# A two-layer Perceiver on one core: the second layer's three blocks run tile by tile side by side, and its fp4 weights are prepared during the first layer

## The chip, the cores and the metric

The kernel runs as one program on one core of a Trainium2 chip. Times are device microseconds (us) of that core. The core has TensorE (PE in the profile, with PEld for its weight loads), VectorE (DVE), ScalarE (ACT), GpSimd (POOL) and SyncE (SP), which here only issues transfers. Each engine executes its own instructions in the order in which the program was written; what couples the engines are semaphores. SBUF is the working memory, PSUM (8 banks of 128 partitions by 512 fp32) takes what TensorE computes.

## What is computed

The latents are 16 sequences of 64 rows of 256 numbers; seen as rows they are 1024, held in `lat` as 8 tiles of 128 rows (two sequences each). The context is 16 sequences of 1024 rows of 256. All attentions have 16 heads of depth 16.

```python
x = x + cross0(layernorm(x), ctx, mask)      # keys and values from the 1024 context rows
x = x + linear_attention(layernorm(x))       # prefix sums of feature maps
x = x + int8_ffn(layernorm(x))
x = x + cross1(layernorm(x), ctx)            # the same without a mask
x = x + causal_attention(layernorm(x))       # over the 64 rows of a sequence
x = x + fp4_ffn(layernorm(x))

# causal_attention: per head softmax(QK^T * scale, causal) V; then
scrambled = cat.transpose(0, 2, 1).reshape(b, s, e)     # cat: the heads side by side
return scrambled @ W_O
# fp4_ffn, with fp4_quant_dequant in blocks of 16 along the last dimension of x and w:
h = silu(q(x) @ q(w_gate).T) * (q(x) @ q(w_up).T)       # 704 wide
return q(h) @ q(w_down).T
```

`q(x)`: scale = max|block|/6, the quotient is rounded to one of the 15 fp4 values and multiplied by the scale again. All blocks work within a sequence, so a tile of two sequences can pass through causal attention and feed-forward as soon as its own cross attention is done.

## The kernel before, in words

Six blocks run one after the other: cross attention of layer 0 (0 to 514 us of the trace), linear attention (to 641), int8 feed-forward (to 706), cross attention of layer 1 (to 1217), causal attention (to 1326), fp4 feed-forward (to the end). Each block is written as one loop per engine.

**Cross attention** (`cross_attention`) is 64 steps s, four to a batch (a context sequence). A step covers four heads of the batch: scores of two half steps into PSUM banks 0 to 3 (`scores`, L502), maxima (DVE, L687), exponentials (ACT, L630), reciprocal of the sums (DVE, L707), multiplication by it (POOL `normalise`, L429), and one step later the transposes of the probabilities in two parts (`transposes`, L512), which ACT (`take_t`, L649) and DVE (L596) copy out in halves. Beside it TensorE projects values two steps ahead (`project_v`, L477, taken by DVE at L660) and keys four steps ahead (`project_k`, L465, taken by ACT at L608); every second step multiplies probabilities by values (`times_v`, L529). Every eight steps, at s = 10, 18, ..., a latent tile is complete: output projection (`output`, L539) and addition into `lat` (DVE, L712).

**PSUM banks.** All of that except the scores goes through banks 4 to 7 in rotation: `cross_plan` walks the steps in TensorE's order and gives each result the next bank. TensorE may write into a bank only once the engine that reads the result four places earlier in the rotation has taken it.

**Fp4 weights.** In layer 1's cross attention DVE also quantises the three feed-forward weights, one of 8 instructions at each of the steps 4 to 33 (with gaps, L174 to L182, 0.7 to 2.0 us each).

**Causal attention and fp4 feed-forward.** `causal_attention` normalises all eight tiles, then goes tile by tile; its scores are computed over 128 keys, those of both sequences of the tile (2048 logits per row and, after masking, half of them zero). `fp4_ffn` normalises and quantises all tiles in two halves, multiplies the weights by their scales on POOL, transposes them on TensorE (36 transposes), and then goes tile by tile: gate and up (L1812), silu (ACT, L1736), product (DVE, L1696), quantisation of the hidden 704 numbers (DVE, L174 to L182 and L1674), six transposes (L1792), down (L1802), addition and store.

## Time and profile before

| | us |
|---|---|
| median of 3 runs | 1435.48 |
| the runs | 1435.47 to 1437.66 |
| the profiled execution | 1439.74 |
| its span in the trace | 1437.8 |
| TensorE busy | 1300.0 (90%) |
| VectorE busy | 939.4 (65%) |
| ScalarE busy | 784.8 (55%) |
| GpSimd busy | 656.6 (46%) |
| layer 1's cross attention | 706 to 1217 |
| causal attention | 1217 to 1326 |
| fp4 feed-forward | 1326 to 1437.8 |

How to read it: the span is the time from the first to the last instruction of the profiled execution; that execution was 2 us longer than its span. The shares are averages over all blocks. The time of a step of cross attention is read from the starts of the score matmuls (L502). PEclk is the clock that TensorE was granted, as a share of 2.4 GHz. A matmul of fp32 leaves two records in the trace for each matmul of the program. A record's duration includes overlap with its neighbours, so paces are taken from the starts of groups that follow each other.

### The profile page before, as it was taken

To read this page: it belongs to the slowest core of one execution; us is meant where nothing else is said; L and a number is where in the kernel's file an instruction comes from. 1 tells how busy PE (TensorE), PEld (TensorE's weight loads), DVE (VectorE), ACT (ScalarE), POOL (GpSimd) and SP (SyncE) were. 2 spreads that over 40 slices of the span, in tenths; PEclk is the share of its full clock that TensorE was granted. 3 is DMA by queue.
4 is the path that set the end of the run, shared out by engine and by line. 5 is a ranking of instruction groups with operands and counts; after the bars stand their busy time and mean duration, and the time that the engine had idled before them with its cause. 6 is when DMAs were issued, how large, how long until landed. Compare 5 with 4: busy or idle time off the path is not lost. (4 is left out here: it accounts for less than half of the span.)

```text
span 1437.8 us, 27154 instructions
## 1 busy us (share of the span) xinstructions
PE 1300.0 (90%) x10721; PEld 895.3 (62%) x10722; DVE 939.4 (65%) x1670; ACT 784.8 (55%) x1315; POOL 656.6 (46%) x351
## 2 busy tenths in 40 slices
PE   6999999999999966965599999999999997897697
PEld 3676676666666644642256666766667665696465
DVE  4656655666556755957657768676566566586886
ACT  4675666666666623534366666666666664354311
POOL 2755566656666522400145556565555555440200
PEclk9999999999999988987699999999999998899798
...
GB/s 159 76 58 45 45 45 45 87 47 45 45 45 45 1 102 0 1 1 0 108 37 31 51 30 31 80 31 31 31 59 31 31 1 24 4 1 1 0 11 19
DMA packets 17085, 55.29 MB, mean 38 GB/s; under 512 B 2753, under 2 KB 8897, under 8 KB 12737
## 3 DMA queue, kind: packets, MB, share of 16 engines
...
## 5 line engine op out<-in xcount | busy, mean ns | idle before, releaser
L429 POOL TENSOR_TENSOR ca_prob<-ca_prob,ca_inv_sum 128x1024 f32<-128x1024 f32 x256 | 493.4, 1948 | 378.4 <-DVE ca_inv_sum L707 378.4
L608 ACT ACTIVATE ca_kT<-bank,ca_bk 64x512 f32<-64x512 f32 x256 | 174.6, 682 | 223.4 <-PE bank L465 221.6
L512 PEld LDWEIGHTS bank<-ident,ca_prob 128*128 128x128 f32 x2048 | 238.4, 141 | 89.4 <-issue 65.7
L512 PE MATMUL bank<-ident,ca_prob 128*128 128x128 f32 x2048 | 266.7, 274 | 9.0 <-POOL ca_prob L429 7.0
L465 PE MATMUL bank<-ca_ctxT,ca_wk 128*128 128x512 f32 x512 | 244.4, 602 | 17.4 <-DMA ca_bk<-in_L_xattn_bk 17.4
L477 PE MATMUL bank<-ca_wv,ca_ctxT 128*128 128x256 f32 x1024 | 254.5, 392 | 0.0
L684 DVE CUSTOM_DVE_ANT_0 ca_neg_logit<-bank,ca_mask_add 128x1024 f32<-128x1024 f32 x128 | 151.6, 1222 | 131.6 <-PE bank L502 95.0
L477 PEld LDWEIGHTS bank<-ca_wv,ca_ctxT 128*128 128x128 f32 x1024 | 184.6, 190 | 82.2 <-issue 62.5
L687 DVE TENSOR_REDUCE ca_neg_max<-bank 128x1 f32<-128x1024 f32 x128 | 150.7, 1219 | 103.3 <-PE bank L502 103.3
L630 ACT ACTIVATE ca_prob<-ca_neg_logit,ca_neg_max 128x1024 f32<-128x1024 f32 x128 | 146.9, 1150 | 62.8 <-DVE ca_neg_max L684 62.8
L630 ACT ACTIVATE ca_prob<-bank,ca_neg_max 128x1024 f32<-128x1024 f32 x128 | 142.5, 1114 | 63.8 <-DVE ca_neg_max L687 63.8
L596 DVE COPY ca_probT<-bank 128x512 f32<-128x512 f32 x256 | 163.7, 681 | 0.7 <-PE bank L512 0.6
L502 PE MATMUL bank<-ca_kT,ca_q_blk 32*128 32x512 f32 x1024 | 146.0, 640 | 2.8 <-DVE ca_v L660 2.7
L649 ACT ACTIVATE ca_probT<-bank 128x512 f32<-128x512 f32 x256 | 139.1, 595 | 14.3 <-PE bank L512 11.3
L465 PEld LDWEIGHTS bank<-ca_ctxT,ca_wk 128*128 128x128 f32 x512 | 89.7, 194 | 84.2 <-issue 66.6
L529 PEld LDWEIGHTS bank<-ca_probT,ca_v 128*32 128x32 f32 x4096 | 108.9, 111 | 49.5 <-issue 32.3
L529 PE MATMUL bank<-ca_probT,ca_v 128*32 128x128 f32 x4096 | 126.2, 276 | 2.9 <-ACT ca_probT L649 2.9
L660 DVE TENSOR_TENSOR ca_v<-bank,ca_bv 128x512 f32<-128x512 f32 x128 | 87.8, 687 | 54.3 <-PE bank L477 54.2
L502 PEld LDWEIGHTS bank<-ca_kT,ca_q_blk 32*128 32x128 f32 x1024 | 40.1, 183 | 30.6 <-issue 28.3
L411 POOL TENSOR_TENSOR ca_q_blk<-q,small 128x512 f32<-128x512 f32 x32 | 33.3, 1040 | 52.7 <-DVE q L668 52.7
L1450 POOL TENSOR_TENSOR sa_q8T<-sa_qT,small 128x2048 f32<-128x2048 f32 x8 | 28.8, 3610 | 41.1 <-PE bank L1488 32.4
L421 POOL TENSOR_SCALAR ca_mask_add<-ca_mask_i 128x1024 f32<-128x1024 int32 x16 | 44.3, 2770 | 0.0
...
## 6 DMA issues: line engine op xcount, KB each, us to landing
...
```

What stands on the lines that cost most here:

```text
L429: pool.tensor_tensor(prob[:, x, :], prob[:, x, :], inv_sum[:, x:x + 1].broadcast_to([P, CTX]), ALU.mult).then_inc(norm_ready, 1)
L465: mm = pe.matmul(bank[:, x, :], wk[:, k, m * P:(m + 1) * P], ctxT[:, b % 2, k, half * HALF_CTX:(half + 1) * HALF_CTX], start=(k == 0), sto ...
L477: mm = pe.matmul(bank[:, x, r * D:(r + 1) * D], ctxT[:, b % 2, k, ch * P:(ch + 1) * P], wv[:, k, :], start=(k == 0), stop=(k == KD - 1))
L502: mm = pe.matmul(bank[:, 2 * j + half, :], q_blk[rows, b % 2, u, :, :], kT[rows, b % 2, u, :], start=True, stop=True, tile_position=(S * h ...
L512: tr = pe.transpose(bank[:, x, n * P:(n + 1) * P], prob[:, 2 * (s % 2) + p, (4 * h + n) * P:(4 * h + n + 1) * P], core.ident[:, :])
L529: mm = pe.matmul(bank[32 * j:32 * j + 32, x, 0:P], v[:, b % 2, ch, m * P + 32 * j:m * P + 32 * j + 32], probT[:, n % 2, ch, j, :], start=( ...
L596: copy(probT[:, n % 2, 4 * h:4 * h + 4, j, :], bank[:, x, :].rearrange("p (n q) -> p n q", q=P)).then_inc(taken[x], 1)
L608: op = act.activation(kT[half * S:(half + 1) * S, b % 2, 2 * m + r, :], bank[r * S:(r + 1) * S, x, :], ACT.Identity, bias=bk[r * S:(r + 1) ...
L630: act.activation(prob[:, y, :], source, ACT.Exp, bias=neg_max[:, y:y + 1], scale=-1.0 if masked else 1.0, accum_out=row_sum[:, y:y + 1]).t ...
L649: take_t(act, lambda out, x: act.activation(out, x, ACT.Copy), s - 1, 1)
L684: dve.tensor_tensor_reduce(neg_logit[:, p, :], scores, mask_add[:, b % 2, :], -1.0, BIG, ALU.add, ALU.min, neg_max[:, y:y + 1]).then_inc(m ...
L687: dve.tensor_reduce(neg_max[:, y:y + 1], scores, AX.X, ALU.max, negate=True).then_inc(max_ready, 1)
```

## The change

The program has three parts now. `first_layer` is cross attention 0 together with everything that the fp4 weights need: DVE quantises the weights at steps 4, 20 and 36 and the seven following, POOL multiplies by the scales eight steps after that start, and TensorE transposes at the steps 10 to 12 after it, three groups of four for each weight. Linear attention and int8 feed-forward stay as they are. `second_layer` is one loop of 82 steps on each engine, of which 0 to 63 are those of the cross attention. `tile_at(s, lag)` gives the latent tile that passes through a stage at step s: tile t is at lag n in step 10 + 8t + n. The stages by lag:

- 0: cross output, addition, statistics of the normalisation (`TileNorm`; ACT takes the root, DVE finishes it in the next step, in front of `take_v`); 1: transposes for causal attention
- 2: q, k, v; POOL spreads the queries. 4: scores and logits, distances from the maximum on POOL. 5: exponentials. 6: transposes. 7: times values, back transposes, division. 8: output and addition, statistics for the feed-forward's normalisation (in step s % 8 == 2 of the next tile; the quantisation of x stands at lag 9)
- 10: transposes for the feed-forward. 11: gate, up, silu, product. 12 and 13: quantisation of the hidden numbers in two parts, then scaling on POOL. 14: six transposes. 15: down, addition, store.

So the last tile passes through its stages in steps 66 to 81, when no cross attention is left beside it. All results of these stages share banks 4 to 7 with the cross attention; `Banks.open` hands out the next bank when TensorE comes to it, and the rule is the one of before (the result four places earlier must have been taken). Causal attention computes only the 64 keys of a row's own sequence: 1024 logits per row in place of 2048, scores and output in TensorE tiles of 64 rows. ScalarE now goes from the exponential to the root, back, to silu and back in each tile: the program has 40 table loads where it had 13. Layer 1's query projections are at steps 28 and 29, and the mask has one buffer instead of two.

In the program order of VectorE, where latent tile 0 becomes complete (end of step 10; L707 is the reciprocal of the sums, L712 the addition, L687 the maxima, L660 the values), stood before:

```order
L660 TENSOR_TENSOR ca_v<-bank,ca_bv 128x512
L596 COPY ca_probT<-bank 128x4x128 x2
L707 RECIPROCAL ca_inv_sum<-ca_row_sum 128x2
L712 TENSOR_TENSOR lat<-bank,lat 128x256
L687 TENSOR_REDUCE ca_neg_max<-bank 128x1 x2
L660 TENSOR_TENSOR ca_v<-bank,ca_bv 128x512
```

and for a later tile stands now, from the same reciprocal on (L663 the addition, L625 the maxima, L607 the values; `tn` is the tile normalisation, `sa` causal attention, `ff` feed-forward):

```order
L663 TENSOR_TENSOR lat<-bank,lat 128x256
L1482 BN_STATS ca_tn_stats<-lat 128x6 x2
L1486 BN_AGGR ca_tn_mv<-ca_tn_stats 128x2 x2
L1488 TENSOR_SCALAR ca_tn_var<-ca_tn_mv 128x2
L625 TENSOR_REDUCE ca_neg_max<-bank 128x1 x2
L1498 RECIPROCAL ca_tn_rstd<-ca_tn_std 128x2
L1501 TENSOR_TENSOR ca_tn_fix<-ca_tn_rstd 128x2
L1503 TENSOR_TENSOR ca_tn_fix<-ca_tn_fix,ca_tn_var 128x2
L1505 TENSOR_SCALAR ca_tn_fix<-ca_tn_fix 128x2
L1507 TENSOR_TENSOR ca_tn_rstd<-ca_tn_rstd,ca_tn_fix 128x2
L1511 TENSOR_SCALAR ca_sa_xn<-lat,ca_tn_mv,ca_tn_rstd 128x256
L1511 TENSOR_SCALAR ca_ff_x<-lat,ca_tn_mv,ca_tn_rstd 128x256
```

The maxima of the next step stand behind five statistics instructions, and seven more stand between them and the values L607, which are the next row.

On TensorE an even step of layer 1's cross attention was, from its scores to the next ones:

```order
L502 MATMUL bank<-ca_kT,ca_q_blk 128x512 x4
L529 MATMUL bank<-ca_probT,ca_v 32x128 x32
L477 MATMUL bank<-ca_wv,ca_ctxT 128x256 x4
L512 MATMUL bank<-ident,ca_prob 128x128 x8
L465 MATMUL bank<-ca_ctxT,ca_wk 128x512 x2
L512 MATMUL bank<-ident,ca_prob 128x128 x8
```

and a step with s % 8 == 0 is now, with the first rows of the step after it (L498 transposes the probabilities of the cross attention, L1595 those of causal attention, L1795 the hidden numbers, L1611 multiplies by the causal values):

```order
L488 MATMUL bank<-ca_kT,ca_q_blk 128x512 x4
L515 MATMUL bank<-ca_probT,ca_v 32x128 x32
L449 MATMUL bank<-ca_wv,ca_ctxT 128x256 x4
L1595 MATMUL bank<-ident,ca_sa_prob 128x128 x4
L1795 MATMUL bank<-ident,ca_ff_hid 128x128 x5
L1795 MATMUL bank<-ident,ca_ff_hid 64x128
L498 MATMUL bank<-ident,ca_prob 128x128 x8
L1595 MATMUL bank<-ident,ca_sa_prob 128x128 x4
L437 MATMUL bank<-ca_ctxT,ca_wk 128x512 x2
L498 MATMUL bank<-ident,ca_prob 128x128 x8
L488 MATMUL bank<-ca_kT,ca_q_blk 128x512 x4
L1611 MATMUL bank<-ca_sa_probT,ca_sa_value 32x64 x32
```

The hidden transposes stand in front of the cross attention's own, and four more results go through the rotation of banks in this step.

GpSimd had the multiplication by the inverse sums and, every fourth step, the queries of the next batch:

```order
L429 TENSOR_TENSOR ca_prob<-ca_prob,ca_inv_sum 128x1024 x2
L411 TENSOR_TENSOR ca_q_blk<-q_1,small 128x512
L429 TENSOR_TENSOR ca_prob<-ca_prob,ca_inv_sum 128x1024 x8
L411 TENSOR_TENSOR ca_q_blk<-q_1,small 128x512
L429 TENSOR_TENSOR ca_prob<-ca_prob,ca_inv_sum 128x1024 x8
```

and has now (L425 the multiplication, L408 the queries, L1688 the spread queries, L1695 the distances, L1876 the scaling of the hidden numbers):

```order
L1688 TENSOR_TENSOR ca_sa_q<-ca_sa_qk,small 128x1024
L425 TENSOR_TENSOR ca_prob<-ca_prob,ca_inv_sum 128x1024 x6
L408 TENSOR_TENSOR ca_q_blk<-ca_q,small 128x512
L1695 TENSOR_TENSOR ca_sa_prob<-ca_sa_prob,ca_sa_top 128x1024
L425 TENSOR_TENSOR ca_prob<-ca_prob,ca_inv_sum 128x1024 x2
L1876 TENSOR_TENSOR ca_ff_hid<-ca_ff_hid,ca_ff_scale 128x704
L425 TENSOR_TENSOR ca_prob<-ca_prob,ca_inv_sum 128x1024 x6
```

The core of the diff:

```diff
+    def open(self, pe, key, bank=None):
+        if bank is None:
+            bank = 4 + self.turn % 4
+            self.turn += 1
+        wait(pe, self.taken[bank], self.count[bank])
+        self.count[bank] += 1
+        self.at[key] = (bank, self.count[bank])
+        return bank
...
+FW_STEPS = (4, 20, 36)
...
+                if 1 <= s <= STEPS:
+                    ca.transposes(pe, s - 1, 0)
+                if s + 4 < STEPS:
+                    ca.project_k(pe, s + 4)
+                if 1 <= s <= STEPS:
+                    ca.transposes(pe, s - 1, 1)
+                for x in range(3):
+                    if 10 <= s - FW_STEPS[x] < 13:
+                        ffn_weights.transposes_on_tensor(pe, x, s - FW_STEPS[x] - 10)
...
+                    ca.queries(pool, s // GROUPS + 1)
+                for x in range(3):
+                    if s == FW_STEPS[x] + 8:
+                        ffn_weights.scale_on_pool(pool, x)
...
+                for x in range(3):
+                    if 0 <= s - FW_STEPS[x] < 8:
+                        ffn_weights.step_on_vector(dve, x, s - FW_STEPS[x])
...
+    def finish_on_vector(self, dve, j, free):
+        c = self.slots(j)
+        dve.wait_ge(self.std_ready, j + 1)
+        dve.reciprocal(self.rstd[:, c], self.std[:, c]).then_inc(self.fix_step, 1)
+        dve.wait_ge(self.fix_step, 5 * j + 1)
+        dve.tensor_tensor(self.fix[:, c], self.rstd[:, c], self.rstd[:, c], ALU.mult).then_inc(self.fix_step, 1)
+        dve.wait_ge(self.fix_step, 5 * j + 2)
+        dve.tensor_tensor(self.fix[:, c], self.fix[:, c], self.var[:, c], ALU.mult).then_inc(self.fix_step, 1)
+        dve.wait_ge(self.fix_step, 5 * j + 3)
+        dve.tensor_scalar(self.fix[:, c], self.fix[:, c], -0.5, 1.5, ALU.mult, ALU.add).then_inc(self.fix_step, 1)
+        dve.wait_ge(self.fix_step, 5 * j + 4)
+        dve.tensor_tensor(self.rstd[:, c], self.rstd[:, c], self.fix[:, c], ALU.mult).then_inc(self.fix_step, 1)
+        dve.wait_ge(self.fix_step, 5 * j + 5)
+        for y in range(c.start, c.stop):
+            free[y](j - y)
+            dve.tensor_scalar(self.outs[y][:, :], self.core.lat[:, j - y, :], self.mv[:, y, 0:1], self.rstd[:, y:y + 1],
+                              ALU.subtract, ALU.mult).then_inc(self.xn_ready[y], 1)
...
+    def output(self, pe, t):
+        self.banks.wait_taken(pe, ("sb", t))
+        x = self.banks.open(pe, ("sy", t))
+        scrambled = self.cat[:, :].rearrange("p (r u) -> p u r", u=4)
+        for u in range(4):
+            for c in range(2):
+                rows = slice(S * c, S * (c + 1))
+                mm = pe.matmul(self.core.bank[rows, x, 0:D], scrambled[rows, u, :], self.w_o[rows, u, :],
+                               start=(u == 0), stop=(u == 3), tile_position=(S * c, S * c))
...
+    def quantise_hidden(self, dve, t, part):
+        if part == 0:
+            for a in range(2):
+                self.banks.wait_taken(dve, ("fu", t, a))
+            dve.wait_ge(self.x_ready, t + 1)
+        steps = fp4_steps(self.hid[:, :], FB, self.mag[:, :], self.scale[:, :], self.inv[:, :], self.hid[:, :],
+                          self.e[:, :])
+        for n in range(4 * part, 4 * part + 4):
+            steps[n](dve).then_inc(self.h_step, 1)
+            dve.wait_ge(self.h_step, 8 * t + n + 1)
+    def scale_hidden(self, pool, t):
+        pool.wait_ge(self.h_step, 8 * (t + 1))
+        grid, scale = fp4_scaled(self.hid[:, :], self.scale[:, :], FB)
+        pool.tensor_tensor(grid, grid, scale, ALU.mult).then_inc(self.h_ready, 1)
...
+def tile_at(s, lag):
+    n = s - 10 - lag
+    return n // 8 if n >= 0 and n % 8 == 0 and n // 8 < TILES else None
...
+            for s in range(END):
+                if s < STEPS:
+                    ca.scores(pe, s)
+                if (t := tile_at(s, 4)) is not None:
+                    sa.scores(pe, t)
+                if s % 2 == 0 and 4 <= s < STEPS + 3:
+                    ca.times_v(pe, s // 2 - 2)
+                if (t := tile_at(s, 7)) is not None:
+                    sa.heads(pe, t)
+                if (t := tile_at(s, 8)) is not None:
+                    sa.output(pe, t)
+                if s + 2 < STEPS:
+                    ca.project_v(pe, s + 2)
+                if (t := tile_at(s, 2)) is not None:
+                    sa.project(pe, t)
+                if (t := tile_at(s, 6)) is not None:
+                    sa.transposes(pe, t, 0)
+                if (t := tile_at(s, 10)) is not None:
+                    ff.latent_transposes(pe, t)
+                if (t := tile_at(s, 11)) is not None:
+                    ff.project(pe, t, 0)
+                if (t := tile_at(s, 14)) is not None:
+                    ff.hidden_transposes(pe, t)
+                if 1 <= s <= STEPS:
+                    ca.transposes(pe, s - 1, 0)
+                if (t := tile_at(s, 6)) is not None:
+                    sa.transposes(pe, t, 1)
+                if s + 4 < STEPS:
+                    ca.project_k(pe, s + 4)
+                if (t := tile_at(s, 7)) is not None:
+                    sa.back(pe, t)
+                if (t := tile_at(s, 11)) is not None:
+                    ff.project(pe, t, 1)
+                if (t := tile_at(s, 15)) is not None:
+                    ff.down(pe, t)
+                if 1 <= s <= STEPS:
+                    ca.transposes(pe, s - 1, 1)
+                if s in Q_STEPS:
+                    ca.project_q(pe, 1, Q_STEPS.index(s))
+                if (t := tile_at(s, 1)) is not None:
+                    sa.latent_transposes(pe, t, attn_xn)
...
+            ca.queries(pool, 0)
+            ca.add_output_bias(pool)
+            for s in range(END):
+                if (t := tile_at(s, 2)) is not None:
+                    sa.spread_queries(pool, t)
+                if s < STEPS:
+                    ca.normalise(pool, s)
+                if s % GROUPS == 2 and s // GROUPS + 1 < B:
+                    ca.queries(pool, s // GROUPS + 1)
+                if (t := tile_at(s, 4)) is not None:
+                    sa.distances(pool, t)
+                if (t := tile_at(s, 13)) is not None:
+                    ff.scale_hidden(pool, t)
...
+            for s in range(END):
+                if s < STEPS:
+                    ca.maxima(dve, s)
+                if s >= 11 and s % 8 == 3 and (s - 11) // 8 <= TILES:
+                    norm.finish_on_vector(dve, (s - 11) // 8, (attn_free, ffn_free))
+                if (t := tile_at(s, 4)) is not None:
+                    sa.logits(dve, t)
+                if s % 2 == 0 and 4 <= s < STEPS + 3:
+                    ca.take_pv(dve, s // 2 - 2)
+                if (t := tile_at(s, 8)) is not None:
+                    sa.take_output(dve, t)
+                if s + 2 < STEPS:
+                    ca.take_v(dve, s + 2)
+                if (t := tile_at(s, 2)) is not None:
+                    sa.take_value(dve, t)
+                if 1 <= s <= STEPS:
+                    ca.take_t_on_vector(dve, s - 1, 0)
+                if (t := tile_at(s, 6)) is not None:
+                    sa.take_transposed_on_vector(dve, t)
+                if s < STEPS:
+                    ca.inverses(dve, s)
+                if (t := tile_at(s, 7)) is not None:
+                    sa.divide(dve, t)
+                if (t := tile_at(s, 11)) is not None:
+                    ff.hidden(dve, t)
+                if (t := tile_at(s, 9)) is not None:
+                    ff.quantise_x(dve, t, ffn_xn)
+                for part in range(2):
+                    if (t := tile_at(s, 12 + part)) is not None:
+                        ff.quantise_hidden(dve, t, part)
+                if (t := tile_at(s, 15)) is not None:
+                    ff.take_output(dve, t)
+                if s == Q_STEPS[1]:
+                    ca.take_q_on_vector(dve, 1)
+                if (t := tile_at(s, 0)) is not None:
+                    ca.take_output(dve, t)
+                if s >= 10 and s % 8 == 2 and (s - 10) // 8 <= TILES:
+                    j = (s - 10) // 8
+                    if j < TILES:
+                        banks.wait_taken(dve, ("o", j))
+                    if j >= 1:
+                        banks.wait_taken(dve, ("sy", j - 1))
+                    norm.stats_on_vector(dve, j)
...
-        cross(core, 0)
+        fp4 = Fp4Weights(core, sb_in(ctx))
+        first_layer(core, fp4)
         with ExitStack() as layer0:
-            weights = Int8Weights(core, sb_in(layer0))
-            linear_attention(core, weights)
-            int8_ffn(core, weights)
-        weights = Fp4Weights(core, sb_in(ctx))
-        cross(core, 1, weights)
-        causal_attention(core)
-        fp4_ffn(core, weights, out)
+            int8 = Int8Weights(core, sb_in(layer0))
+            linear_attention(core, int8)
+            int8_ffn(core, int8)
+        second_layer(core, fp4, out)
```

## Rows read from the trace of the kernel before

**Rows 1.** The page: busy us, share of the span and instructions by engine.
```profile
PE 1300.0 (90%) x10721; PEld 895.3 (62%) x10722; DVE 939.4 (65%) x1670; ACT 784.8 (55%) x1315; POOL 656.6 (46%) x351
```
**Rows 2.** Stretches: length, busy us of PE, PEld, DVE, ACT, POOL; PEclk, DMA.
```profile
735.00:1208.00 473.00, 469.32 (x4247) 323.24 (x4248) 318.15 (x475) 302.47 (x506) 269.69 (x144) 1.00 0.10 35
1217.00:1326.00 109.00, 92.05 (x794) 79.96 (x795) 76.81 (x97) 47.94 (x67) 33.52 (x11) 0.92 0.04 10
...
1340.00:1358.00 18.00, 9.24 (x30) 6.12 (x31) 17.00 (x20) 4.90 (x11) 0.00 (x0) 0.63 0.00 0
1358.00:1438.00 80.00, 70.13 (x271) 47.66 (x270) 58.87 (x88) 13.88 (x34) 0.00 (x0) 0.93 0.04 14
```
**Rows 3.** Timeline of PE, steps 10 and 11: start, duration, idle before in brackets.
```profile
803.11 1.14 PE L502 MATMUL bank<-ca_kT,ca_q_blk 32*128 32x512 f32 x8
...
808.77 1.88 PE L465 MATMUL bank<-ca_ctxT,ca_wk 128*128 128x512 f32 x4
810.49 1.04 PE L512 MATMUL bank<-ident,ca_prob 128*128 128x128 f32 x8
...
812.32 1.14 PE L502 MATMUL bank<-ca_kT,ca_q_blk 32*128 32x512 f32 x8
...
818.57 1.16 PE L512 MATMUL bank<-ident,ca_prob 128*128 128x128 f32 x8 [0.59 <-DVE ca_v L660]
819.66 1.14 PE L502 MATMUL bank<-ca_kT,ca_q_blk 32*128 32x512 f32 x8
```
**Rows 4.** Timeline of PE: scores of steps 34, 42 and 63.
```profile
987.09 1.14 PE L502 MATMUL bank<-ca_kT,ca_q_blk 32*128 32x512 f32 x8
...
1047.18 1.14 PE L502 MATMUL bank<-ca_kT,ca_q_blk 32*128 32x512 f32 x8
...
1199.98 1.14 PE L502 MATMUL bank<-ca_kT,ca_q_blk 32*128 32x512 f32 x8
```
**Rows 5.** Groups of instructions, 735 to 1208 us: count, busy us, mean ns, idle before.
```profile
L429 POOL TENSOR_TENSOR ca_prob<-ca_prob,ca_inv_sum 128x1024 f32<-128x1024 f32 x128 | 253.7, 2003 | 203.3 <-DVE ca_inv_sum L707 203.3
L687 DVE TENSOR_REDUCE ca_neg_max<-bank 128x1 f32<-128x1024 f32 x128 | 150.7, 1219 | 103.3 <-PE bank L502 103.3
L660 DVE TENSOR_TENSOR ca_v<-bank,ca_bv 128x512 f32<-128x512 f32 x62 | 42.5, 686 | 28.4 <-PE bank L477 28.4
```
**Rows 6.** Timeline of PE in causal attention, one tile's part.
```profile
1277.46 1.95 PE L1488 MATMUL bank<-sa_kT,sa_q8T 128*128 128x128 f32 x16
1279.25 1.04 PE L1524 MATMUL bank<-ident,sa_prob 128*128 128x128 f32 x8
1280.12 1.20 PE L1499 MATMUL bank<-sa_w_o,sa_cat_pad 128*128 128x256 f32 x4
1281.16 1.04 PE L1524 MATMUL bank<-ident,sa_prob 128*128 128x128 f32 x8
```
**Rows 7.** Timeline of PE in the fp4 feed-forward, from tile to tile.
```profile
1403.03 0.82 PE L1792 MATMUL bank<-ident,ff_hq 128*128 128x128 f32 x6
...
1411.40 0.82 PE L1792 MATMUL bank<-ident,ff_hq 128*128 128x128 f32 x6
```
**Rows 8.** Groups of instructions, 1326 to 1438 us.
```profile
L181 DVE SCALAR_TENSOR_TENSOR ff_hid<-ff_hid,ff_h_e 128x704 f32<-128x704 f32 x8 | 7.1, 893 | 0.3
L179 DVE TENSOR_SCALAR ff_h_e<-ff_hid 128x704 int32<-128x704 int32 x8 | 4.2, 527 | 0.3
```
**Rows 9.** Timeline of DVE and POOL at a weight's quantisation.
```profile
785.47 1.74 DVE L177 TENSOR_TENSOR ca_fw_raw<-ca_fw_raw,ca_fw_inv 128x1536 f32<-128x1536 f32 x1
785.63 5.18 POOL L429 TENSOR_TENSOR ca_prob<-ca_prob,ca_inv_sum 128x1024 f32<-128x1024 f32 x2 [3.02 <-DVE ca_inv_sum L707]
```
**Rows 10.** Timeline of PE in the feed-forward's first transposes.
```profile
1349.20 1.94 PE L1759 MATMUL bank<-ident,ff_xq 128*128 128x128 f32 x8 [7.27 <-DVE ff_xq L1674]
```

**Rows 11.** Timeline of ACT before the feed-forward's first silu.
```profile
1351.18 1.09 ACT L1714 ACTIVATE xnT<-bank 128x512 f32<-128x512 f32 x2 [8.57 <-PE bank L1759]
1352.28 1.28 ACT L1736 ACT_TABLE_LOAD   x1
```

1660 lines of the change are left out of this document (845 added, 815 removed).

## The prediction, made before the run

> **What bounds the kernel now.** I read the page's busy shares first: TensorE is busy 90% of the span and no other engine over 65% [rows 1]. Then the windows by block [rows 2]: through layer 1's cross attention TensorE is busy 469 of 473 us at full clock, while DVE is busy 318, ACT 302 and POOL 270. TensorE alone sets the time there, and its gaps total 4 us. In the blocks behind it TensorE is busy 92 of 109 us, 9 of 18 and 70 of 80, and the granted clock falls to 0.63 of full speed in one stretch. The change moves the work of the blocks with gaps into the one without. So the idle TensorE time of those three stretches (17 + 9 + 10 = 36 us, and some of the 14 us between the first two) is all that can be won by overlap; beside it there is work that falls away, and new waits are what can be lost.
>
> The clock of the cross attention is its steps. Eight steps take 1047.18 - 987.09 = 60.1 us [rows 4]; a step that ends with the output projection takes 9.21, 803.11 to 812.32 [rows 3]. One row shows how the rotation of banks bites: at 818.57 TensorE waited 0.59 us for DVE's value copy, in a step of 7.34 us [rows 3]. The values' bank must be free four results later, and DVE had been held by a weight's quantisation.
>
> **The change, part by part.**
>
> *First layer.* It gains 36 weight transposes of 128 columns. The pace is 16 records in 1279.25 - 1277.46 = 1.79 us, 0.11 each [rows 6], so 3.9 us on a TensorE that is as full as in layer 1. DVE's 24 quantisation instructions are the ones that layer 1 had, three POOL multiplications of 1536 elements are new (3 us each by L429's 2.0 for 1024, [rows 5]), and I add 1.4 us for one bank wait and for switches: +5.3 (3.9 if all is hidden, 9 if each weight costs two waits like the one at 818.57). Layer 1 loses that wait: -1.0. Linear attention and int8 feed-forward: 0.
>
> *TensorE work that moves into steps 10 to 62, causal attention, per tile.* 14 transposes at 0.109 = 1.5; 12 records of projections at 0.112 = 1.3; 32 score records of 64 columns at half of 0.112 = 1.8 (0.9 if the two 64-row tiles run side by side); 64 records times values, 0.6; output, 16 records of 256 columns, 1.04 for four [rows 6], in two 64-row tiles side by side, 1.9 (4.2 one after the other). Sum 7.2, and 0.6 for switches between tile shapes: 7.8. *Feed-forward, per tile:* 1411.40 - 1403.03 = 8.37 from tile to tile with TensorE full [rows 7], plus two transposes: 8.6. In steps 10 to 62 fall six causal tiles and the first part (3.4) of a seventh, 50.2, and five feed-forward tiles with gate and up of a sixth (5.1), 48.1. Together 98.3 us, all of it on the path, since TensorE has no gap to take it.
>
> *Waits in those steps.* In the eight-step pattern I followed DVE, ACT and POOL in program order against TensorE's bank requests. DVE waits 103.3 us for score matmuls over 64 steps [rows 5], so it has 1.6 us to spare before the maxima of an average step, and the added groups are longer than that:
> - Step 3 of 8: five statistics instructions and the addition stand before the maxima, about 1 us late; then the finish, five small operations and two of 256 elements, 1.95 us, stands before the values copy (0.69, [rows 5]), whose bank is wanted by the probabilities' transposes: 1.9 us lost.
> - Step 4: quantising x, 3.4 us at the end of step 3, delays the maxima: 0.7.
> - Step 5: the silu needs a table load, 1.28 [rows 11], while it holds the gate's two banks: 0.4.
> - Step 0: the hidden quantisation is five operations like L181's 0.893, two like L179's 0.527 and small ones, 5.5 us in two parts [rows 8]. When DVE works on SBUF operands POOL's multiplication slows: two that normally take 2.0 each [rows 5] took 5.18 together beside a DVE multiplication [rows 9]. POOL has distances (1.9), two multiplications stretched by 0.6 each and then the scaling (1.3) in its queue, and the hidden transposes stand before the cross attention's on TensorE: 1.75.
> - Step 1: the bank of the causal heads waits for ACT, behind the exponentials: 1.2.
>
> Sum 5.95 per eight steps, over six patterns: 35.6 us. Below, it is nothing (every late copy has a bank to spare); above, twice this, 71, if each late operation also delays the next step. I take the walk, since 818.57 shows that a bank wait really falls on TensorE whole. So eight steps become 60.1 + 7.8 + 8.6 + 5.95, about 82.4.
>
> A row on ACT: the load at 1352.28 starts 0.01 us after the copy before it ends and takes 1.28 [rows 11]; no row shows an activation right behind a load. I count 1.28 for each of the four loads per tile.
> By the Trainium skill (ScalarE: Activation LUTs, What ACT_TABLE_LOAD costs), a switch to another set takes about 1.38 us of drain beside the 1.28. By that rule ACT would be 5.5 us busier per tile, and two of these drains would stand before exponentials or the silu that TensorE waits for; the sum would be some 13 us higher. The trace agrees on 1.28 and can't show the rest.
>
> *The tail.* Step 63 starts at 1199.98 [rows 4], and 237.8 us follow before. Now what follows is the last cross steps (about 17 us, as before: causal attention began at 1217, [rows 2]), and then one tile that passes alone through everything. Its chain, from durations of the same operations: normalisation and transposes 5.4, projections to exponential 11.1, to the second addition 6.7, normalisation and quantisation 7.7, gate to product 5.4, hidden quantisation and scaling 6.5, transposes to store 7, so 50, and some 7 for hand-overs. Tile 6's feed-forward stands in the same queues, 16 more. That is 90 with TensorE warm. Cold, eight transposes took 1.94 us [rows 10] against 0.87 warm (1279.25 to 1280.12, [rows 6]), so the 22 us of matmuls in that stretch could double, 112. In the comparable sparse stretch the clock was 0.63 [rows 2], half way: 102.
>
> *Sum.* 1200.0 + 5.3 - 1.0 + 98.3 + 35.6 + 102 = 1440.2 us of span against 1437.8, +2.4. The profiled execution (1439.74) stands 4.3 above the median; on the median's scale the change gives 1435.5 + 2.4, about 1438.
>
> **The rivals.**
>
> *A. The waits are hidden, TensorE stays full.* For it: DVE would be busy some 57 and POOL some 42 of 82 us in eight steps, so nobody but TensorE is near full, and before the waits totalled 4 us in 473 [rows 2]. Against it: the added DVE groups come in lumps of 2 to 3.4 us, over the 1.6 of slack. Price: -35.6, so 1402 on the median's scale; with half of them, 1420.
>
> *B. Slower: late copies chain.* DVE stands late at the maxima in four successive steps (2 to 5), and every maxima 1 us late puts the exponentials, POOL's multiplication and the next step's transposes late as well; POOL's wait for inverses (203.3 us over 64 steps, 3.2 each, [rows 5]) shows that this chain has only little of its step left over. It decides where the lump exceeds 1.6 us in steps without a gap between. The waits would be doubled (+35.6), 1474 on the median's scale, and with half of the doubling 1456. Against it: the odd steps without added work let the queues recover.
>
> *C. Slower: small TensorE tiles don't run side by side.* The rows show eight 32-row records of 512 columns in about 1.1 us [rows 3], against 1.72 for four full ones (808.77 to 810.49, [rows 3]), so 32-row tiles do overlap; no row has 64-row tiles. If they run one after the other, the output costs 2.3 more per tile and the values 0.6 to 3: about 4, over seven tiles 28, so 1466.
> The Trainium skill (TensorEngine Tiling (Array Packing), Key Properties) says tiles operate independently, and that changing the mode drains TensorE. The first half speaks for my 1.9, the second for a larger term than my 0.6 for switches: there are eight to ten changes per tile, and no row here prices one apart from its neighbours.
>
> **How the numbers follow.** My walk: 0.47, centred on 1438, its own range 1422 to 1454 (tail 90 to 112, first layer 3.9 to 9, scores at 0.9). A: 0.28. B: 0.15. C: 0.10. The range reaches from A's 1402 to B's 1474 with little left outside. A comparison of this kernel can't tell differences under about 0.2% (3 us). Faster by more: all of A, 0.28, and the third of my case that lies below 1432.5, 0.15: 0.43. Within 0.2%: 0.14 from my case. Slower: 0.18 from my case, 0.25 from B and C: 0.43.
>
> **What would show it.** In the trace after: eight steps of layer 1 take 82.4 us (76.5 under A, 88 under B); TensorE's idle time there is put down to DVE's values and normalisation in steps 3 and 4, to POOL's scaling in step 0 and to ACT's heads in step 1; 16 causal output records take 1.9 us (4.2 under C); the first layer is 5 us longer; from step 63 to the end it is 102 us with a clock below 0.9. I am wrong in my main step if TensorE is over 98% busy in steps 20 to 60, and in the tail if that lasts under 90 or over 112 us.

## The result and the profile after

The changed kernel takes 1483.59 us (median of 4 runs, 1481.89 to 1485.6) against 1436.47 before in the same comparison: a ratio of 1.0328, 95% interval 1.031 to 1.0346. It is 3.3% slower, outside the range given (1402 to 1474). The profiled execution has a span of 1483.5 us; the forecast was 1440.2 on that scale.

Below are the busy times from the page, then windows with the columns of [rows 2]. The first window is layer 2's loop up to step 63, the second eight steps, the third the tail, the fourth a part of step 44. Where the text names a step 0 to 7, it is the step's number modulo 8, so that step 44 is a step 4:

```profile
PE 1299.6 (88%) x11025; PEld 880.9 (59%) x11026; DVE 968.6 (65%) x1762; ACT 798.5 (54%) x1345; POOL 674.6 (45%) x366
```
```profile
737.00:1377.00 640.00, 590.83 (x5264) 407.29 (x5264) 435.54 (x690) 361.37 (x603) 288.40 (x158) 0.97 0.08 25
1137.00:1226.00 89.00, 81.59 (x724) 56.32 (x722) 62.31 (x97) 48.21 (x82) 37.97 (x22) 0.96 0.08 26
1377.00:1484.00 107.00, 62.16 (x493) 45.20 (x492) 49.79 (x96) 22.68 (x41) 18.43 (x10) 0.71 0.01 4
1168.70:1173.30 4.60, 4.60 (x73) 2.78 (x72) 4.43 (x6) 0.59 (x2) 3.45 (x2) 0.63 0.00 0
```

TensorE had 4 us idle in 473 before [rows 2] and has 49 in 640 now, at a clock of 0.97 in place of 1.00. TensorE's busy total is as before (1300), though causal attention computes half the scores: part of it ran at half clock.

TensorE's timeline of after in eight steps, from step 41 (1137.09) to step 49 (1226.12); it answers to [rows 3, 4]. Start, duration, waits in brackets:

```profile
1137.09 1.14 PE L488 MATMUL bank<-ca_kT,ca_q_blk 32*128 32x512 f32 x8
...
1151.72 2.00 PE L1634 MATMUL bank<-ca_sa_w_o,ca_sa_cat 64*64 64x256 f32 x16
1153.66 1.99 PE L449 MATMUL bank<-ca_wv,ca_ctxT 128*128 128x256 f32 x8
...
1167.20 1.16 PE L498 MATMUL bank<-ident,ca_prob 128*128 128x128 f32 x8 [1.63 <-DVE ca_v L607]
1168.39 0.41 PE L1552 MATMUL bank<-ident,ca_sa_xn 128*128 128x128 f32 x2
1168.73 2.09 PE L488 MATMUL bank<-ca_kT,ca_q_blk 32*128 32x512 f32 x8
...
1177.38 0.41 PE L1774 MATMUL bank<-ident,ca_ff_x 128*128 128x128 f32 x2 [0.74 <-DVE ca_attnT L649]
...
1194.54 2.00 PE L1583 MATMUL bank<-ca_sa_qk,ca_sa_q 64*128 64x64 f32 x32
1196.47 1.95 PE L515 MATMUL bank<-ca_probT,ca_v 128*32 128x128 f32 x64
...
1218.74 0.66 PE L1795 MATMUL bank<-ident,ca_ff_hid 128*128 128x128 f32 x4 [2.15 <-POOL ca_ff_hid L1876]
1220.18 0.69 PE L1795 MATMUL bank<-ident,ca_ff_hid 128*128 128x128 f32 x2 [0.78 <-DVE ca_attnT L649]
1220.87 1.94 PE L498 MATMUL bank<-ident,ca_prob 128*128 128x128 f32 x8
...
1226.12 1.14 PE L488 MATMUL bank<-ca_kT,ca_q_blk 32*128 32x512 f32 x8
```

Eight steps take 89.0 us. The waits in them add to 7.4 (with four smaller ones that aren't shown: 0.84, 0.72, 0.33 and 0.19). Behind two of the waits TensorE ran at half clock: the scores at 1168.73 took 2.09 where the same group at 1137.09 took 1.14, with a granted clock of 0.63 in that window, and eight transposes took 1.94 at 1220.87 in place of 1.04. The wait alone doesn't decide it: of the five waits of 1.63 for the values between 800 and 1320 us only three were followed by slow scores.

Where the time went, by the starts of the score matmuls, forecast beside it: up to step 10 of layer 2 (805.97 against 803.11) +2.9 for +5.3; steps 10 to 63, 571.0 for 396.9, that is +174.1 for 132.9; from step 63 (1376.96) to the end 106.5 for 102. Nearly the whole miss, 41 of 43 us, lies in the steps 10 to 63. Of the 174.1, 98.3 are the forecast TensorE work, 1.7 is a query projection that the change moves in from step 8 (step 8 was 10.07 long before, 8.35 now), and 74.1 are put down to waits and half clock, where the forecast had 35.6. (Some of it is neither: in e1, below, TensorE is busy 77.4 us in eight steps at full clock, and the forecast was 76.5, so about 0.9 per eight steps, some 6 us in all, are work that the forecast lacked.)

Why DVE is late is read in its own timeline at the start of step 4, with GpSimd's instructions beside it:

```profile
1168.24 0.40 DVE L173 TENSOR_REDUCE ca_ff_mag<-ca_ff_x 128x16 f32<-128x256 f32 x1
1168.40 3.75 POOL L425 TENSOR_TENSOR ca_prob<-ca_prob,ca_inv_sum 128x1024 f32<-128x1024 f32 x2 [5.86 <-DVE ca_inv_sum L658]
1168.67 1.65 DVE L174 TENSOR_SCALAR ca_ff_scale<-ca_ff_mag 128x16 f32<-128x16 f32 x1
1170.36 0.25 DVE L175 RECIPROCAL ca_ff_inv<-ca_ff_scale 128x16 f32<-128x16 f32 x1
1170.64 1.78 DVE L176 TENSOR_TENSOR ca_ff_x<-ca_ff_x,ca_ff_inv 128x256 f32<-128x256 f32 x1
1172.46 0.29 DVE L178 TENSOR_SCALAR ca_ff_e<-ca_ff_x 128x256 int32<-128x256 int32 x1
...
1174.38 1.22 DVE L625 TENSOR_REDUCE ca_neg_max<-bank 128x1 f32<-128x1024 f32 x1
```

An operation on 16 numbers took 1.65 us, and one on 256 took 1.78. Alone they take 0.17 and 0.42 (e3, below, has them so), so their work lay behind 1170.15 and behind 1172.00. These points are 1.85 apart, the length of one of GpSimd's two multiplications, and stand 0.12 and 0.15 before the ends of these by the profile (1168.40 + 1.87 = 1170.27, and 1172.15). The reciprocal between them took 0.25, as in e1, so it was not delayed. The quantisation stands right behind the reciprocal of the sums, which releases GpSimd's multiplications: by the order of the program the two always meet. It also goes the other way. Here GpSimd's queries for the next batch, which take 1.04 us where nothing holds them (at 1161.50), take 1.69 beside the last 0.8 us of a DVE multiplication:

```profile
1204.92 2.06 DVE L176 TENSOR_TENSOR ca_ff_hid<-ca_ff_hid,ca_ff_inv 128x704 f32<-128x704 f32 x1
1206.19 1.69 POOL L408 TENSOR_TENSOR ca_q_blk<-ca_q,small 128x512 f32<-128x512 f32 x1
```

The quantisation's operations by their means over the whole kernel after, and the variance of the tile normalisation (count, busy us, mean ns):

```profile
L180 DVE SCALAR_TENSOR_TENSOR ca_ff_hid<-ca_ff_hid,ca_ff_e 128x704 f32<-128x704 f32 x8 | 16.6, 2072 | 0.3
L176 DVE TENSOR_TENSOR ca_ff_hid<-ca_ff_hid,ca_ff_inv 128x704 f32<-128x704 f32 x8 | 14.1, 1768 | 0.3
L179 DVE TENSOR_SCALAR ca_ff_e<-ca_ff_e 128x704 f32<-128x704 f32 x8 | 13.7, 1706 | 0.3
L176 DVE TENSOR_TENSOR ca_ff_x<-ca_ff_x,ca_ff_inv 128x256 f32<-128x256 f32 x8 | 11.5, 1441 | 0.3
L1859 DVE TENSOR_TENSOR ca_ff_hid<-bank,ca_ff_hid 128x352 f32<-128x352 f32 x16 | 8.4, 524 | 34.3 <-PE bank L1784 34.3
L173 DVE TENSOR_REDUCE ca_ff_mag<-ca_ff_hid 128x44 f32<-128x704 f32 x8 | 6.9, 868 | 0.1
L1488 DVE TENSOR_SCALAR ca_tn_var<-ca_tn_mv 128x2 f32<-128x2 f32 x7 | 6.2, 890 | 0.2
```

L180 took 893 ns before (as L181, [rows 8]) and L179 took 527 (as L180, like its neighbour in [rows 8]); now they take 2072 and 1706. The product L1859, which has one operand in PSUM, took 524 also where nothing else was slow (e1), and the reduction took 869 there: these two are not slower. The variance takes 890 ns, where an operation of its form and size (L1505) takes 169: it stands beside GpSimd's queries.

### The profile page after: what moved, and what is told of

Same layout as the page of the kernel before. It is cut to its first block, busy times and chain, and to the rows that moved or that the text cites. A ratio compares the mean times of both kernels' runs of the same rounds, so it can differ in the third digit from the quotient of the medians.

```text
span 1483.5 us, 27972 instructions
## 1 busy us (share of the span) xinstructions
PE 1299.6 (88%) x11025; PEld 880.9 (59%) x11026; DVE 968.6 (65%) x1762; ACT 798.5 (54%) x1345; POOL 674.6 (45%) x366
## 4 chain that ended last, share of the span: by engine, by line
PE 30%; DVE 14%; issue 6%; ACT 2%; DMA 0%; POOL 0%; POOLq 0%; DVEq 0%; SPq 0%; ACTq 0%
PE bank L437 6%; PE bank L498 6%; PE bank L449 4%; DVE ca_neg_max L625 4%; PE bank L488 3%; PE bank L515 2%; PE bank L1784 2%; PE bank L1806 1%; DVE ca_probT L635 1%; DVE ca_v L607 1%; DVE ca_ff_scale L174 1%; PE bank L1634 1%; PE bank L1583 1%; DVE ca_ff_hid L180 1%; DVE ca_ff_e L179 1%
## 5 line engine op out<-in xcount | busy, mean ns | idle before, releaser
L425 POOL TENSOR_TENSOR ca_prob<-ca_prob,ca_inv_sum 128x1024 f32<-128x1024 f32 x256 | 494.7, 1954 | 459.6 <-DVE ca_inv_sum L658 459.6
L498 PEld LDWEIGHTS bank<-ident,ca_prob 128*128 128x128 f32 x2048 | 240.3, 143 | 115.9 <-issue 83.4
L498 PE MATMUL bank<-ident,ca_prob 128*128 128x128 f32 x2048 | 276.0, 278 | 28.9 <-DVE ca_v L607 17.3
L437 PE MATMUL bank<-ca_ctxT,ca_wk 128*128 128x512 f32 x512 | 250.1, 614 | 23.3 <-DMA ca_bk<-in_L_xattn_bk 19.7
L625 DVE TENSOR_REDUCE ca_neg_max<-bank 128x1 f32<-128x1024 f32 x128 | 150.6, 1218 | 89.5 <-PE bank L488 89.1
L607 DVE TENSOR_TENSOR ca_v<-bank,ca_bv 128x512 f32<-128x512 f32 x128 | 87.7, 686 | 44.4 <-PE bank L449 44.3
L408 POOL TENSOR_TENSOR ca_q_blk<-ca_q,small 128x512 f32<-128x512 f32 x32 | 41.0, 1282 | 55.2 <-DVE ca_q L598 55.2
L1688 POOL TENSOR_TENSOR ca_sa_q<-ca_sa_qk,small 128x1024 f32<-128x1024 f32 x8 | 15.2, 1895 | 64.1 <-ACT ca_sa_qk L1651 64.1
```

Source lines behind the costliest of these rows:

```text
L425: pool.tensor_tensor(self.prob[:, x, :], self.prob[:, x, :], self.inv_sum[:, x:x + 1].broadcast_to([P, CTX]), ALU.mult).then_inc(self.norm ...
L437: mm = pe.matmul(self.core.bank[:, x, :], self.wk[:, k, m * P:(m + 1) * P], self.ctxT[:, b % 2, k, half * HALF_CTX:(half + 1) * HALF_CTX], ...
L498: tr = pe.transpose(self.core.bank[:, x, n * P:(n + 1) * P], self.prob[:, 2 * (s % 2) + p, (4 * h + n) * P:(4 * h + n + 1) * P], self.core ...
L625: dve.tensor_reduce(self.neg_max[:, y:y + 1], scores, AX.X, ALU.max, negate=True).then_inc(self.max_ready, 1)
```

## The experiments

Theory H: DVE instructions with two SBUF inputs, and tensor_scalar ones on SBUF, are held until GpSimd's running instruction ends. (Held means: by the profile the instruction has started, and its work comes only later.) The held time makes the maxima and the hidden numbers late. Rival W: DVE is late from the work alone, which comes in lumps longer than its slack. All times are medians: of eight executions for e1, of four for v2_repeat and v3, of two for the others. The kernel before, measured beside each of them, took 1437 to 1441. A waits figure is steps 10 to 63 less 396.9, 98.3 and 1.7, as above.

### e1_reduce: the same work in forms that are not held

```diff
+def fp4_like(x, blocks, mag, scale, inv, y, e):
+    xb = x.rearrange("p (n k) -> p n k", k=HD)
+    half = x[:, 0:blocks // 2 * HD].rearrange("p (n k) -> p n k", k=HD)
+    full = lambda v: v.tensor_reduce(e[:, 0:blocks], xb, AX.X, ALU.max)
+    part = lambda v: v.tensor_reduce(e[:, 0:blocks // 2], half, AX.X, ALU.max)
+    return [
+        lambda v: v.tensor_reduce(mag, xb, AX.X, ALU.max, apply_absolute_value=True),
+        lambda v: v.reciprocal(scale, mag),
+        lambda v: v.reciprocal(inv, scale),
+        full, part, part, full, full,
+    ]
...
-        steps = fp4_steps(self.hid[:, :], FB, self.mag[:, :], self.scale[:, :], self.inv[:, :], self.hid[:, :],
+        steps = fp4_like(self.hid[:, :], FB, self.mag[:, :], self.scale[:, :], self.inv[:, :], self.hid[:, :],
```

> What is changed: in layer 2's tile-by-tile feed-forward the fp4 quantisation of x and of the hidden numbers is replaced by as many DVE instructions of about the same length that are single-input reductions or reciprocals (the numbers are not quantised). Theory H (DVE's two-input and tensor_scalar operations on SBUF are held until GpSimd's running multiplication ends; held time 8 us per eight steps): these forms are not held, eight steps fall from 89.0 to about 83, the time from 1483.6 to about 1449. Rival W (DVE is late only because of the work itself): the same work stands in the same places, time 1475 to 1484.

The kernel doesn't quantise these numbers, so its result is another one.

Measured: 1427.98 us, ratio to before 0.9943 (0.9918 to 0.9968). Its reductions of 704 and 256 numbers and eight steps of its trace:

```profile
L189 DVE TENSOR_REDUCE ca_ff_e<-ca_ff_hid 128x44 f32<-128x704 f32 x24 | 21.3, 886 | 0.8
L189 DVE TENSOR_REDUCE ca_ff_e<-ca_ff_x 128x16 f32<-128x256 f32 x24 | 10.1, 420 | 0.8
```
```profile
1042.00:1131.00 89.00, 86.18 (x816) 61.17 (x807) 59.06 (x106) 51.69 (x87) 38.51 (x22) 1.00 0.08 26
```

The work is as long as the original's unheld durations (886 for 892, 420 for 425), stands in the same places, and TensorE is busy 86 of 89 us again at full clock. Eight steps fell from 89.0 to 80.2, below the 83 that I expected, since the half clock went with the waits. Step 63 starts at 1326.7 in place of 1377.0, and the waits are 22.8 in place of 74.1. So 51 us of the loss in steps 10 to 63 are holds of the quantisation and what they bring, and W is wrong. 22.8 is what my walk, which had 35.6, should be set against. One hold is left in e1: the variance still takes 889 ns, and TensorE's wait for the values in step 3 is still 1.6 us.

### e2_no_quant: the quantisation left out

```diff
-        for n in range(4 * part, 4 * part + 4):
-            steps[n](dve).then_inc(self.h_step, 1)
-            dve.wait_ge(self.h_step, 8 * t + n + 1)
+        if part == 1:
+            dve.wait_ge(self.h_step, 8 * t)
+            dve.reciprocal(self.scale[:, :], self.mag[:, :]).then_inc(self.h_step, 8)
```

> What is changed: the fp4 quantisation of x and of the hidden numbers on DVE is left out (one reciprocal stands for each). Both theories: the waits of steps 4, 7 and 0 go, those of step 3 (normalisation finish, 2.4 us) and step 1 (heads, 1.1) stay; eight steps about 80, and the tail 12 to 15 us shorter: 1420. If H holds, e1 reaches most of the way inside the cross attention (eight steps within 3 us of this one); if W holds, e1 stays 8 us per eight steps above it.

Measured: 1414.08 us, ratio 0.984 (0.9809 to 0.9871). Step 63 starts at 1327.3, 0.6 us from e1's 1326.7. With about 8 us of DVE work more per tile e1 loses nothing inside the cross attention (steps 10 to 63 take 519.7 in both). The 14 us between the two lie behind step 63 (85.9 against 99.9), where the work is on the last tiles' chain.

### e3_before_inverses: the quantisation ahead of the instruction that releases GpSimd

```diff
+                if (t := tile_at(s, 9)) is not None:
+                    ff.quantise_x(dve, t, ffn_xn)
+                for part in range(2):
+                    if (t := tile_at(s, 12 + part)) is not None:
+                        ff.quantise_hidden(dve, t, part)
                 if s < STEPS:
                     ca.inverses(dve, s)
...
-                if (t := tile_at(s, 9)) is not None:
-                    ff.quantise_x(dve, t, ffn_xn)
-                for part in range(2):
-                    if (t := tile_at(s, 12 + part)) is not None:
-                        ff.quantise_hidden(dve, t, part)
```

> What is changed: the same DVE instructions, but the quantisation stands in front of the reciprocal of the sums that releases GpSimd's multiplication, not behind it. H: GpSimd is idle then, nothing is held; the multiplication starts 2.4 to 3.1 us later, which step 4 hides, step 7 does not (about +2) and step 0 half: eight steps about 85, time 1461. W: moving the same work ahead of the reciprocal only adds lateness to GpSimd's chain: 1483 to 1500.

Measured: 1460.4 us, ratio 1.0162 (1.0121 to 1.0204), as H expected (1461): the same instructions, 23 us less than the changed kernel. In its trace:

```profile
L179 DVE TENSOR_SCALAR ca_ff_e<-ca_ff_e 128x704 f32<-128x704 f32 x8 | 12.1, 1515 | 0.3
L180 DVE SCALAR_TENSOR_TENSOR ca_ff_hid<-ca_ff_hid,ca_ff_e 128x704 f32<-128x704 f32 x8 | 7.1, 892 | 0.3
L176 DVE TENSOR_TENSOR ca_ff_hid<-ca_ff_hid,ca_ff_inv 128x704 f32<-128x704 f32 x8 | 7.1, 892 | 0.3
```

Most forms have their own durations again; L179 of the hidden numbers, and with it L178 (1025 ns, where it took 510 in after), still come out long, and I read that as meeting GpSimd's work of the step before. Step 4 fell from 12.95 to 10.1. Step 0 stayed at 13.7 to 15.3: there the hidden transposes still wait for quantisation and scaling.

### e4_hid_late: the hidden transposes at the end of their step

```diff
-                if (t := tile_at(s, 14)) is not None:
-                    ff.hidden_transposes(pe, t)
                 if 1 <= s <= STEPS:
                     ca.transposes(pe, s - 1, 0)
...
+                if (t := tile_at(s, 14)) is not None:
+                    ff.hidden_transposes(pe, t)
```

> What is changed against the changed kernel: the hidden numbers' transposes stand at the end of step 0 on TensorE, behind the cross attention's own (and their copies on ACT behind the cross attention's), nothing else. H (held DVE instructions make the quantisation late, and the transposes that wait for it hold everything behind them): step 0 falls from 14.9 to about 11, since GpSimd's scaling ends before the step does; 5 patterns, 1463. Rival: the exponentials and their chain are late in step 0 anyway and the wait moves to the cross attention's transposes: 1478 to 1484.

Measured: 1481.25 us, ratio 1.0289 (1.0234 to 1.0344): the rival was right. Step 0 is 15.3 long:

```profile
1218.60 0.65 PE L498 MATMUL bank<-ident,ca_prob 128*128 128x128 f32 x4 [3.15 <-DVE ca_attnT L649]
```

The wait has moved to the cross attention's own transposes, whose bank must be freed by a DVE instruction (L649) that stands behind maxima, which stand behind the held quantisation. GpSimd's scaling, which the trace of after names at 1218.74 and on which my step 0 rested, was only the first of two late things. So the 1463 that I drew from H missed.

### e5_pool_halves: how long a hold lasts

```diff
-            pool.tensor_tensor(self.prob[:, x, :], self.prob[:, x, :], self.inv_sum[:, x:x + 1].broadcast_to([P, CTX]),
-                               ALU.mult).then_inc(self.norm_ready, 1)
+            for h in range(2 if self.layer else 1):
+                w = CTX // (2 if self.layer else 1)
+                c = slice(w * h, w * (h + 1))
+                op = pool.tensor_tensor(self.prob[:, x, c], self.prob[:, x, c],
+                                        self.inv_sum[:, x:x + 1].broadcast_to([P, w]), ALU.mult)
+            op.then_inc(self.norm_ready, 1)
```

> What is changed against the changed kernel: GpSimd's multiplication of layer 2's probabilities is issued as four instructions of 512 columns instead of two of 1024. H: a held DVE instruction waits until GpSimd's running instruction ends, so holds halve (256-element multiplication 1.78 us to about 1.1, 704-element 2.06 to about 1.5); 8 us of held time become 4, time about 1463. Rival R (the two engines share a port's rate and slow each other while both run): no instruction of DVE gets shorter, 1483 to 1488.

Measured: 1460.24 us, ratio 1.0143 (1.0089 to 1.0198), H's 1463; R had 1483 to 1488. Means in its trace:

```profile
L428 POOL TENSOR_TENSOR ca_prob<-ca_prob,ca_inv_sum 128x512 f32<-128x512 f32 x228 | 243.5, 1099 | 240.4 <-DVE ca_inv_sum L662 240.3
```
```profile
L180 DVE SCALAR_TENSOR_TENSOR ca_ff_hid<-ca_ff_hid,ca_ff_e 128x704 f32<-128x704 f32 x8 | 11.4, 1430 | 0.3
L176 DVE TENSOR_TENSOR ca_ff_hid<-ca_ff_hid,ca_ff_inv 128x704 f32<-128x704 f32 x8 | 9.0, 1127 | 0.3
L176 DVE TENSOR_TENSOR ca_ff_x<-ca_ff_x,ca_ff_inv 128x256 f32<-128x256 f32 x8 | 6.4, 801 | 0.3
```

The 256-number multiplication is held 0.38 us over its own 0.42, in place of 1.02; the 704-number ones 0.2 to 0.5 in place of 0.9 to 1.2. The length of GpSimd's instruction sets the hold. More instructions meet one, since GpSimd has more of them (L178 of x rose from 294 to 834 ns, L181 of the hidden numbers from 892 to 1431), but the sum falls: over the quantisation and the variance from 7.0 to 4.4 us per tile. The steps that gain are step 0 (14.9 to between 12.6 and 14.3), step 7 (7.46 to 6.46) and step 3 (8.82 to 8.11, with the variance at 279 ns in place of 890); step 4 stays at about 12.7.

### e6_finish_late: the normalisation's finish behind the copies

```diff
-                if s >= 11 and s % 8 == 3 and (s - 11) // 8 <= TILES:
-                    norm.finish_on_vector(dve, (s - 11) // 8, (attn_free, ffn_free))
...
                     sa.take_transposed_on_vector(dve, t)
+                if s >= 11 and s % 8 == 3 and (s - 11) // 8 <= TILES:
+                    norm.finish_on_vector(dve, (s - 11) // 8, (attn_free, ffn_free))
```

> What is changed against the changed kernel: the normalisation's finish (seven DVE instructions, 1.7 us) stands behind the copies of values and probabilities in step 3. Theory: the wait of 1.63 us for the values' bank goes; the normalised tile is there 1.3 us later and TensorE waits for it at the end of the step instead, about 1: step 3 falls from 8.82 to about 8.2, time 1475 to 1480. Rival: the bank wait was due to the maxima being late, not to the finish: step 3 stays 8.8.

Measured: 1490.9 us, ratio 1.0356 (1.0292 to 1.042). Step 3 fell from 8.82 to 8.43, but step 4, 12.8 to 14.7 in after, is 13.3 to 16.8. Both parts of my expectation miss. TensorE in step 4:

```profile
1182.92 0.41 PE L1774 MATMUL bank<-ident,ca_ff_x 128*128 128x128 f32 x2 [2.74 <-DVE ca_attnT L649]
...
1184.96 3.05 PE L437 MATMUL bank<-ca_ctxT,ca_wk 128*128 128x512 f32 x4
```

DVE's queue from the latent addition to the end of x's quantisation holds the same instructions as before, so TensorE waits for its end, at step 4, in one wait of 2.74 us in place of 1.63 and 0.74 at two places. Behind the longer one the key projection ran at 3.05 us in place of 1.88. My reading is that a wait spared at one place of a queue that is late as a whole comes back at the next one; no run here tests it apart.

### v1_spread and v2_spread: a schedule after H

```diff
+                if (t := tile_at(s, 10)) is not None:
+                    ff.quantise_x(dve, t, ffn_xn, 0)
                 if s + 2 < STEPS:
                     ca.take_v(dve, s + 2)
...
+                if s >= 11 and s % 8 == 3 and (s - 11) // 8 <= TILES:
+                    norm.finish_on_vector(dve, (s - 11) // 8, (attn_free, ffn_free))
+                if (t := tile_at(s, 11)) is not None:
+                    ff.quantise_x(dve, t, ffn_xn, 1)
+                if (t := tile_at(s, 14)) is not None:
+                    ff.quantise_hidden(dve, t, 1, 4)
+                if (t := tile_at(s, 15)) is not None:
+                    ff.quantise_hidden(dve, t, 4, 8)
                 if s < STEPS:
                     ca.inverses(dve, s)
...
+                if (t := tile_at(s, 13)) is not None:
+                    ff.hidden(dve, t)
+                    ff.quantise_hidden(dve, t, 0, 1)
```

This is v2's loop of DVE, where quantise_hidden takes the range of its eight instructions. Gate and up are in step 7 of the eight, the hidden transposes in step 3, down in step 5. v1 has x's first part behind `take_v`; what else v2 adds stands in its expectation.

> What is changed: a reordering of layer 2's loop after H. The norm's finish stands behind the value and probability copies; x is quantised in two parts (steps 4 and 5 of 8, the second ahead of the reciprocal), the gate and up move to step 7, the hidden numbers are quantised in three parts (steps 7, 0, 1, ahead of the reciprocal), their transposes come at the end of step 3 and down in step 5; the cross output stands before the transposes, the causal heads are taken before the exponentials on ACT. H: eight steps about 78, T63 about 1313, tail 108: 1421. W: the total of DVE work is unchanged; if it was the work, the lateness moves to other steps: 1460 or more.

Measured: 1422.96 us, ratio 0.9902 (0.9873 to 0.993); step 63 at 1328.6 (expected 1313), tail 92 (expected 108). The total comes within 2 us of the 1421 expected by luck: two errors of mine, 16 us each, cancel. Under W it would have been 1460 or more.

> What is changed against v1_spread: gate stands behind the key projection and up behind the transposes in step 7, with the silu behind ACT's key copy; the hidden transposes before the key projection in step 3; the first part of x's quantisation before the values copy in step 4 (GpSimd idle); the fp4 weights of the first layer one step later, so that a cheap instruction of them meets the latent addition. v1 lost 2.0 us in each of the steps 3 and 7 and 1.0 in step 4 against TensorE's own work. If these three are what I take them for, eight steps fall from 81.3 to about 77.5, time about 1402; if the waits only move, 1415 to 1423.

Measured: 1397.2 us, ratio 0.9705 (0.964 to 0.977), where 1402 was expected. It changes four things at once, so what each is worth is not shown.

> The same kernel as v2_spread, timed in three rounds: 1394 to 1400, ratio to the kernel before 0.97 to 0.975.

Measured: 1395.46 us (1393.71 to 1399.55), ratio to before 0.9708, interval 0.9683 to 0.9733: 2.9% faster than before and 5.9% faster than the changed kernel. TensorE's waits in 90 us of the loop (waited for, us in total, times, longest), and two of the formerly held instructions:

```profile
PE bank L1784 <- ACT ca_ff_hid L1824: 0.7, 1, 0.7
PE bank L498 <- ACT ca_ff_hidT L1831: 0.2, 1, 0.2
PE bank L437 <- DVE ca_probT L635: 0.2, 1, 0.2
```
```profile
L180 DVE SCALAR_TENSOR_TENSOR ca_ff_hid<-ca_ff_hid,ca_ff_e 128x704 f32<-128x704 f32 x8 | 7.1, 893 | 0.3
L179 DVE TENSOR_SCALAR ca_ff_e<-ca_ff_e 128x704 f32<-128x704 f32 x8 | 4.2, 527 | 0.3
```

Eight steps take 78.0 us, and the tail is 87.5. Steps 10 to 63 take 1304.0 - 803.1 = 500.9; gate and up of the sixth tile now fall behind step 63 (5.1 less), so the waits are 500.9 - 396.9 - 93.2 - 1.7 = 9.1. In eight steps TensorE is busy 76.9 of the 78.0 us, so again a part of that is work and not waiting.

### v3_spread_halves: the two remedies together

The edit of e5 on v2.

> What is changed against v2_spread: GpSimd's multiplication in layer 2 as four instructions of 512 columns in place of two of 1024, as in e5_pool_halves. Theory H: v2_spread has hardly any held instruction left (the norm's variance, 0.4 us too long per eight steps), so the halves bring back next to nothing, and GpSimd's queue is 0.15 to 0.3 us longer per step: within 3 us of v2_repeat. Rival (the smaller instructions help by themselves, because the first transposes can start earlier): 5 us or more below it.

Measured: 1398.92 us, ratio 0.9727 (0.9705 to 0.975), 3.5 us above v2_repeat with overlapping intervals. Eight steps are 0.3 longer (78.3). With hardly any holds left (the variance is the longest, 571 ns in v2_repeat), the halves have nothing to give.

## Why the prediction was wrong, step by step

- **First layer**: +5.3 forecast. Step 63 of layer 0 starts at 504.33 in place of 498.09, +6.2, within the range given (3.9 to 9). Up to step 10 of layer 2 it is +2.9, that is +4.6 at step 0 less the 1.7 that moved. It is known to some 3 us: in e1 to e6, whose first layer is the same code, layer 2's step 0 starts at 734.2 to 739.4 (737.3 in after).
- **TensorE work per tile**: nearly right, 77.4 us in e1's eight steps and 76.9 in v2's for 76.5. The causal output, 16 records, took 1.94 us (1151.72 to 1153.66; 1.9 forecast), the scores 1.93 (1194.54 to 1196.47; 1.8), gate, up and down 2.36, 2.36 and 2.88. Rival C is wrong: the 64-by-64 tiles of the output run side by side, at 0.12 a record where full ones took 0.26 [rows 6]; on this point the Trainium skill (TensorEngine Tiling (Array Packing), Key Properties) and the trace agree. What a change of tile shape costs was not measured apart; with my 0.6 for them the sum is 0.4 to 0.9 us short per eight steps, so they come to 1.0 to 1.5 if the other terms are right (an estimate). The 32 score records came at 0.060 each, no better than one after another.
- **The step that failed: "Waits in those steps", 5.95 per eight steps, and in it the sentence on DVE and GpSimd in step 0.** I read [rows 9] as a slowing of GpSimd's multiplication, put a price on that side alone (0.6 per multiplication), and in one step. The term was 35.6 us and came out at 74.1. The runs show an exclusion that works both ways. The row says so if it is worked out: DVE's instruction ran from 785.47 to 787.21, GpSimd's pair, issued at 785.63, took 5.18 where a pair takes 3.75 (1168.40 above); the 1.4 more is about the 1.6 that DVE still had to run. In the changed kernel the side that waits is mostly DVE, and DVE's lateness is what TensorE waits for. By steps, against TensorE's own work: step 4 lost 3.0 (0.7 forecast), step 0 5.0 (1.75), step 7 1.0 (none), step 3 2.0 (1.9), step 1 1.1 (1.2), step 5 0.6 (0.4). The three that are off are the three behind a quantisation: 9.0 us per eight steps for a forecast of 2.45, while steps 3, 1 and 5 lost 3.7 for a forecast of 3.5. e1 brings step 4 to 0.3 and steps 7 and 0 to nothing. In step 3 the agreement is in part luck, since the walk counted the held variance as a short instruction: in e5, where it takes 279 ns, step 3 loses only 1.3.
- **The clock**: the forecast had none of it outside the tail. Of the 8.8 us per eight steps that the holds cost (89.0 against e1's 80.2), 4.2 are half clock: TensorE is busy 81.6 us in after and 77.4 in e1 (1108.79 to 1189.03).
- **The table loads**: the Trainium skill (ScalarE: Activation LUTs, What ACT_TABLE_LOAD costs) adds a drain of about 1.38 us to each. The trace of after doesn't show it; an exponential starts 0.02 us behind the load. The trace of before could have said so: an activation starts 0.01 us behind the load at 645.36. Leaving the 13 us out of the sum was right:

```profile
1162.82 1.28 ACT L568 ACT_TABLE_LOAD   x1
1164.12 1.11 ACT L568 ACTIVATE ca_prob<-bank,ca_neg_max 128x1024 f32<-128x1024 f32 x1
```

- **The tail**: 106.5 for 102, at a clock of 0.71 (1377 to 1484); the bounds 90 to 112 hold.
- **The rivals**: B is the one that came true in kind (late copies chain), and its point, lumps over the slack of 1.6 us, is too simple: e1 has the same lumps without the loss. It gave 1474, 10 us short, and had a chance of 0.15; its 88 us for eight steps is close to the 89.0, but for another cause. A, no waits, was attainable: v2 is at 1395, below A's 1402, with the same layer 2 work on TensorE, by another order of the instructions.
